# Every second context add moved from VectorE to GpSimd, and a window's input normalized in one pass, in a fused attention and feed-forward kernel

## The reference

```python
scores = jnp.einsum('nlcd,nled->nldce', q, k) / Kk ** 0.5
attn = jax.nn.softmax(scores, axis=-1)
ctx = jnp.einsum('nldcm,nlcd->nldm', attn, v)
ctx = ctx.transpose(0, 1, 3, 2)
out = jnp.einsum('nlck,ko->nlco', ctx, Wout) + bout
...
gated = jax.nn.silu(gate) * up
return jnp.einsum('bsh,dh->bsd', gated, w_down)
...
x = x + _layernorm(_L0_attn_ref(_layernorm(x, axis=-1), L0_attn_Wqkv, L0_attn_bqkv, L0_attn_Wout, L0_attn_bout), axis=-1)
x = x + _layernorm(_L0_ffn_ref(_layernorm(x, axis=-1), L0_ffn_w_gate, L0_ffn_w_up, L0_ffn_w_down), axis=-1)
```

## Time and profile before

| what | us |
|---|---|
| runs of the kernel before, median of 2 | 6556.85 (6422.88 and 6690.82) |
| profiled execution, its own time | 6414.95 |
| span of the profiled core (first to last instruction) | 6413.4 |
| spans of the 8 cores | 6396.5 to 6413.4 |
| VectorE busy | 3232.0 |
| TensorE busy | 3143.4 |
| ScalarE busy | 2046.3 |

### The profile page before, as it was taken

The page is one execution under the profiler, slowest core; times in us unless marked ns, Lnnn a source line. Parts: engine busy times, 40 slices in busy tenths (PEclk is TensorE's granted clock), DMA queues, the critical chain, the costliest instruction groups (busy, mean ns, idle before and its releaser), DMA issues.

```text
span 6413.4 us, 47482 instructions; the slowest of 8 cores (6396.5 to 6413.4 us)
## 1 busy us (share of the span) xinstructions
PE 3143.4 (49%) x15293; PEld 1477.7 (23%) x15544; DVE 3232.0 (50%) x3780; ACT 2046.3 (32%) x2977; POOL 16.4 (0%) x34
## 2 busy tenths in 40 slices
...
GB/s 111 110 109 108 110 102 0 7 5 2 17 20 138 73 141 79 129 79 32 75 137 69 132 95 102 67 48 95 103 100 97 125 79 66 53 145 137 154 138 82
DMA packets 177941, 556.83 MB, mean 87 GB/s; under 512 B 49568, under 2 KB 65952, under 8 KB 174496
## 3 DMA queue, kind: packets, MB, share of 16 engines
...
...
## 4 chain that ended last, share of the span: by engine, by line
PE 30%; DVE 27%; another core or an unknown queue 15%; issue 12%; ACT 10%; DMA 6%; DVEq 1%; SPq 0%; ACTq 0%
PE dps L415 10%; PE gps L353 9%; PE ups L363 7%; DVE es_sb L321 6%; DMA wd_sb<-wdc 4%; DVE zs_sb L762 4%; DVE es_sb L747 4%; DVE zs_sb L756 3%; DVE ctx_sb L330 3%; ACT kd_sb L262 2%; DMA x2s_sb<-x2h 2%; PE mps L189 1%; ACT v_sb L299 1%; ACT q_sb L299 1%
## 5 line engine op out<-in xcount | busy, mean ns | idle before, releaser
L353 PE MATMUL gps<-xn_sb,wg_sb 128*128 128x512 bf16 x4008 | 935.1, 384 | 104.5 <-DVE gated_sb L388 88.1
L415 PE MATMUL dps<-gated_sb,wd_sb 128*128 128x512 bf16 x4013 | 920.1, 384 | 93.5 <-DMA wd_sb<-wdc 54.3
L784 ACT ACTIVATE es_sb<-es_sb 128x4096 bf16<-128x4096 bf16 x256 | 922.1, 3602 | 8.8 <-DVE es_sb L747 8.8
L363 PE MATMUL ups<-xn_sb,wu_sb 128*128 128x512 bf16 x4016 | 920.3, 379 | 4.2
L249 PE MATMUL mps<-xn_sb,wqkv_sb 128*128 128x128 bf16 x512 | 72.3, 302 | 1437.6 <-DVE xn_sb L815 1386.4
L202 DVE TENSOR_SCALAR st_sb<-mps 1x128 f32<-1x128 f32 x48 | 13.3, 278 | 1429.5 <-PE mps L189 1429.5
L773 ACT ACTIVATE rz_sb<-zf_sb 128x128 bf16<-128x128 bf16 x256 | 79.0, 309 | 1855.0 <-DVE zf_sb L766 1854.8
L321 DVE TENSOR_TENSOR es_sb<-es_sb,u_sb 128x4096 bf16<-128x4096 bf16 x256 | 586.8, 2292 | 28.0 <-DVE u_sb L312 1.8
L747 DVE TENSOR_TENSOR es_sb<-q_sb,kd_sb 128x4096 bf16<-128x4096 bf16 x256 | 584.9, 2286 | 8.7 <-DVE ctx_sb L326 0.5
L330 DVE TENSOR_TENSOR ctx_sb<-ctx_sb,es_sb 128x4096 bf16<-128x4096 bf16 x240 | 550.1, 2292 | 24.9
L353 PEld LDWEIGHTS gps<-xn_sb,wg_sb 128*128 128x128 bf16 x4096 | 399.1, 99 | 611.4 <-issue 157.9
...
## 6 DMA issues: line engine op xcount, KB each, us to landing
wg_sb<-wgc SPq DMA_DIRECT2D x256, 512.0 KB, 3.7
wu_sb<-wuc SPq DMA_DIRECT2D x256, 512.0 KB, 3.7
wd_sb<-wdc SPq DMA_DIRECT2D x256, 512.0 KB, 3.4
...
```

The lines of the kernel that those rows point to most:

```text
L353: return tn.matmul(out=gps[pb].ap(), lhsT=wg_sb[pb].ap()[:, ft * 128:(ft + 1) * 128], rhs=xn2_sb.ap()[:, ft * W:(ft + 1) * W], start=(ft = ...
L363: return tn.matmul(out=ups[pb].ap(), lhsT=wu_sb[pb].ap()[:, ft * 128:(ft + 1) * 128], rhs=xn2_sb.ap()[:, ft * W:(ft + 1) * W], start=(ft = ...
L415: return tn.matmul(out=dps[pb].ap(), lhsT=wd_sb[wb].ap()[:, sh * 128:(sh + 1) * 128], rhs=gated_sb.ap()[:, ht * W:(ht + 1) * W], start=(ht ...
L784: ta = plan.op("A", lambda a, buf=buf: a.activation(out=buf.ap(), in_=buf.ap(), func=AF.Exp, scale=0.125), deps=[last[f"s_{c}_{j}"]], inc="A")
```

## The change

Three things are edited.

First, in `emit_uP` the add into `ctx_sb` of odd j is put into POOL's list; even j stay with VectorE. Each add still depends on the one before, and whatever reads the sum depends on it.

Second, the broadcast of the second normalization's rows is no longer made per chunk. VectorE copies the two rows of a chunk into `a2b2_w`, and the broadcast is made once for the whole window, two matmuls of 128x512 and two ScalarE evictions.

Third, `emit_xn2prep_early` and `emit_xn2prep_late` are replaced by one `emit_xn2prep`, called where the late part was. It loads all four quarters from `x2h` behind the spill of the window's last chunk and then runs 16 pairs of operations, each on 512 tokens.

```diff
@@ emit_uP
-        eng = "V"
+        eng = "V" if j % 2 == 0 else "G"
...
-    def emit_xn2prep_early(w):
+    def emit_xn2prep(w):
+        te = None
+        for half, dst in ((0, a2bc_sb), (1, b2bc_sb)):
+            b = next_mbank()
+            tk = plan.op("T", lambda tn, half=half, b=b: tn.matmul(
+                out=mps[b].ap()[:, 0:W], lhsT=ones_r.ap(),
+                rhs=a2b2_w.ap()[0:1, half * W:(half + 1) * W],
+                start=True, stop=True),
+                deps=dep(f"pm{b}") + [last[f"a2b2_{w}"]], inc="T")
+            te = plan.op("A", lambda a, b=b, dst=dst: a.activation(
+                out=dst.ap(), in_=mps[b].ap()[:, 0:W], func=AF.Copy),
+                deps=[tk] + dep("a2bcfree"), inc="A")
...
             def d_r(s, w=w, k=k):
                 src = x2h.rearrange("(fp p) tok -> p fp tok", p=128)[
-                    :, k:k + 1, w * W:w * W + 3 * T]
+                    :, k:k + 1, w * W:(w + 1) * W]
...
-            d = dep("xn2_free") + [last[f"spill_c{CPW * w + CPW - 2}"]]
+            d = dep("xn2_free") + [last[f"spill_w{w}"]]
             if k >= 4:
                 d.append(trs[k - 4])
             trs.append(plan.op("S", d_r, deps=d, inc=f"Dxr{k % 4}"))
...
-    def emit_xn2prep_late(w):
...
-            tk2 = plan.op("T", lambda tn, b=b: tn.matmul(
-                out=mps[b].ap()[:, 0:2 * T], lhsT=ones_r.ap(),
-                rhs=ab_row.ap(), start=True, stop=True),
-                deps=dep(f"pm{b}", "ones") + [t2], inc="T")
...
+            tcp = plan.op("V", lambda v, cl2=cl2: v.tensor_copy(
+                out=a2b2_w.ap()[0:1, cl2 * T:(cl2 + 1) * T],
+                in_=ab_row.ap()[0:1, 0:T]), deps=[t2] + dep("a2b2free"),
+                inc="V")
...
         if 0 <= c - 1 < NC and (c - 1) % CPW == CPW - 1:
-            emit_xn2prep_late((c - 1) // CPW)
+            emit_xn2prep((c - 1) // CPW)
...
-        if 0 <= c < NC and c % CPW == CPW - 1:
-            emit_xn2prep_early(c // CPW)
```

More of the change, by code:

```diff
@@ L539, in emit_fin @@
         last["outsfree"] = tw
-    def emit_xn2prep_early(w):
+    def emit_xn2prep(w):
[10 more added lines that the diff above has]
+                deps=[tk] + dep("a2bcfree"), inc="A")
+            last[f"pm{b}"] = te
+        ab2bc = te
+        last["a2b2free"] = te
         trs = []
@@ L554, in emit_xn2prep_early @@
         tv = None
-        abdep = [last[f"a2bc_{CPW * w + i}"] for i in range(CPW - 1)]
         for k in range(NFT):
-            xn2r = xn2_sb.ap()[:, k * W:k * W + 3 * T]
+            xn2r = xn2_sb.ap()[:, k * W:(k + 1) * W]
             tv = plan.op("V", lambda v, xn2r=xn2r: v.tensor_mul(
-                out=xn2r, in0=xn2r, in1=a2bc_sb.ap()[:, 0:3 * T]),
-                deps=[trs[k]] + abdep, inc="V")
+                out=xn2r, in0=xn2r, in1=a2bc_sb.ap()),
+                deps=[trs[k], ab2bc], inc="V")
             tv = plan.op("V", lambda v, xn2r=xn2r: v.tensor_sub(
-                out=xn2r, in0=xn2r, in1=b2bc_sb.ap()[:, 0:3 * T]),
-                deps=[tv], inc="V")
-        for i in range(CPW - 1):
-            last[f"a2bcfree{i}"] = tv
-    def emit_xn2prep_late(w):
-        cl = CPW - 1
-        xcv = x2c_sb.ap().rearrange("p (f t) -> p f t", f=NFT)
-        xnv = xn2_sb.ap().rearrange("p (f w) -> p f w", f=NFT)[
-            :, :, cl * T:(cl + 1) * T]
-        tcp = plan.op("V", lambda v, xnv=xnv, xcv=xcv: v.tensor_copy(
-            out=xnv, in_=xcv),
-            deps=dep("xn2_free") + [last[f"x2_{CPW * w + cl}"]], inc="V")
-        last["x2c_free2"] = tcp
-        tv = None
-        for k in range(NFT):
-            xn2r = xn2_sb.ap()[:, k * W + cl * T:k * W + (cl + 1) * T]
-            tv = plan.op("V", lambda v, xn2r=xn2r: v.tensor_mul(
-                out=xn2r, in0=xn2r,
-                in1=a2bc_sb.ap()[:, cl * T:(cl + 1) * T]),
-                deps=[tcp, last[f"a2bc_{CPW * w + cl}"]], inc="V")
-            tv = plan.op("V", lambda v, xn2r=xn2r: v.tensor_sub(
-                out=xn2r, in0=xn2r,
-                in1=b2bc_sb.ap()[:, cl * T:(cl + 1) * T]),
-                deps=[tv], inc="V")
-        last[f"a2bcfree{cl}"] = tv
+                out=xn2r, in0=xn2r, in1=b2bc_sb.ap()), deps=[tv], inc="V")
+        last["a2bcfree"] = tv
         last[f"xn2_{w}"] = tv
@@ L675, in build_program @@
                 out=x23, in0=xb3, in1=sq3, op=ALU.add),
-                deps=[tv] + dep("x2c_free", "x2c_free2")
-                + [last[f"xb{cp}"]], inc="V")
+                deps=[tv] + dep("x2c_free") + [last[f"xb{cp}"]], inc="V")
             last["ao_free"] = tv
```

21 lines of the change are left out of this document (7 added, 14 removed).

## The result

The changed kernel took 6917.56 us (median of 11 runs, 6831.57 to 7003.31) against 6416.87 us (10 runs) before. The ratio is 1.0683, 95% interval 1.064 to 1.0725, 6.8% slower; it leaves out the executions in which some cores showed a lower TensorE clock and took a few per cent longer, as the two medians don't.

A forecast was written before the change was run, and what follows sets the result against it. The prediction took VectorE's in-order stream as the chain in nearly all of slots 0 to 15. Its terms summed to +494 us on the profiled execution's 6415 us, giving 6909 us, 7.7% slower, with an 8-in-10 range of 6550 to 7250 us.

The forecast's parts named there:

- The hold: Odd attention steps: next score product waits 9.2 us for POOL's add; +188 attention alone, +117 gate/up, +70 last odd steps.
- Rival B: POOL's add takes 5.5 us, the unpacked rate, so gate/up steps hide it; +145 us, 6560 us; chance 15%.
- C: Not slower: POOL adds at VectorE's rate, 2.3 us; 6371 us together; chance 5%.
- The two engines together: VectorE operations on two SBUF tiles beside POOL's add: cost taken midway between undisturbed and one behind the other; +45 and +35 us.
- slot ends: Step 15's POOL add beside xn1's two operations at 15 ends: between -2.3 and +6.9 us each, middle +2.3, +35 us.
- output steps: Twelve steps with fin operations beside POOL's add: between +1 or less and +6.9 us each, 3.7 taken, +45 us.
- rival A: VectorE work on two SBUF tiles and a POOL add exclude each other; +6.9 us per place, 7016 us; chance 28%.
- Steps with down atoms: Eighteen feed-forward down-projection steps beside attention: slack nearly hides POOL's add, 1.0 us charged each, +18 us.
- Broadcast: No broadcast per chunk: ScalarE is free sooner, 12 slot ends that aren't a window's come 1.9 us earlier, -23 us.
- One-pass preparation: xn2 prepared in one piece behind the window's last chunk: +4.5 us at each of 4 windows, +14 us together.
- TensorE's clock: 39 odd gate/up steps: longer idling drops the clock to 1.2 GHz in one of three, 13 x 1.8, +23 us.
- Rival D: TensorE stays at 1.2 GHz for every whole odd gate/up step, 28.0 us each; 7268 us; chance 7%.

The follow-up runs named there:

- run 3: The changed kernel with only the add of each slot's last step, step 15, back on VectorE; ratio to the kernel before 1.0538.
- run 7: The kernel before with only the chunk's broadcast emitted behind the next chunk's sums, at the 12 slot ends closing no window; ratio to before 0.9967.

## Why the prediction came out right, step by step

The direction and the size were right: +494 us predicted, +424 measured, 6909 us against 6838.6 for the profiled execution, with the mechanism named as the largest term in its place. But two of its sizes were off in opposite directions, and what I gave 28% as a rival is what happens.

- **The hold.** Right in mechanism, mis-sized in its price. I took POOL's add as 8.93 us, from an f32 operation of VectorE on 128 elements; it takes 7.93 us, and with the hand-over 8.2. That a row of VectorE on 128 elements came within 13% of it was luck, since no row tied the two engines. With this number the prediction's own subtractions give 5.7, 2.0 and 4.8 us (8.2 less 2.5, 6.2 and an average of 3.4 between P and the next score product); measured are 5.65, 1.98 and 4.92. One wrong microsecond, 79 times, is 79 of the 375 us of these three terms. Rival B, 5.5 us, falls with this number, and so does C.
- **The two engines together.** This was the open place, and I took the middle between undisturbed and shut out, at the slot ends and at the output steps. The middle was wrong: it is the full exclusion, rival A. Slot ends cost 5.2 us each in place of 2.3, 42 us more, and run 3 shows it by taking away the neighbour. The output steps cost 5.0 and not 3.7. With the add at 7.93, A's own 6.9 us become 5.9 (8.2 less 2.3). The slot ends stay 0.7 under that since L792 and the hand-over to POOL overlap: the add that stood for L792 is only 0.8 us longer (the 8757 ns above) than one that stood for nothing. The rule stood in the prediction, with rival A: the Trainium skill, page "SBUF — State Buffer", section "Who interferes with whom", says that a VectorE instruction with two SBUF inputs and a GpSimd instruction that reads SBUF shut each other out for the whole instruction. By that rule the trace agrees, with 8.74 us for L796, and with L383, which reads one operand from PSUM, at most 0.69. The middle between the ends left 56 us out.
- **Steps with down atoms.** I had +18, measured are -14. The even steps gave back 64 us and the odd ones took 50: TensorE runs through such steps at its own pace, and the late VectorE catches up in the next. That the slack of two steps is one account is what I wrote; I then charged 1.0 us a step all the same.
- **Broadcast.** -23 predicted, -22 in the changed kernel and -24.6 in run 7. That the sums wait for ScalarE's square, and this for the two evictions, held.
- **One-pass preparation.** +4.5 us a window predicted, +7.9 measured. The step that failed: I let the last load set the end, with two operations behind it. VectorE at the end of window 0:

```profile
2086.70 0.42 DVE L571 TENSOR_TENSOR xn_sb<-xn_sb,a2bc_sb 128x512 bf16<-128x512 bf16 x1 [3.41 <-DMA xn_sb<-x2h]
2087.23 0.42 DVE L574 TENSOR_TENSOR xn_sb<-xn_sb,b2bc_sb 128x512 bf16<-128x512 bf16 x1
...
2100.34 0.42 DVE L574 TENSOR_TENSOR xn_sb<-xn_sb,b2bc_sb 128x512 bf16<-128x512 bf16 x1
2100.68 0.27 DVE L202 TENSOR_SCALAR st_sb<-mps 1x128 f32<-1x128 f32 x1
```

and SyncE's queue there:

```profile
2076.21 0.36 SPq L689 DMA_DIRECT2D x2h<-x2c_sb  x1
2081.98 12.24 SPq L561 DMA_DIRECT2D xn_sb<-x2h  x16
```

  VectorE waits once, for the first load, and then needs 14.0 us for its own 32 operations (2086.70 to 2100.68), more than the 12.2 in which the loads are issued. It is 24.5 us from the spill to L202, where I had 20.3 (1903.67 to 1924), worked out from the queue of the earlier trace rows. What I had forecast as waits of about 10 us at L571 is one of 3.4. (By its own rows the prediction's weight loads would be issued from 1920.4 on and not from 1920.8; nothing hangs on it.)
- **TensorE's clock.** +23 predicted, about nothing measured. The drops came, more often than I said: in the steps of slots 4 to 15 TensorE idled 25 times for 3.0 to 5.5 us ahead of gate/up or down matmuls, and 24 times the granted clock fell to 0.50 for a short while, late in the stretch or within 1.3 us behind it. One of them in the timeline, and the window of 4 us around it (PEclk is the third number from the end):

```profile
2165.82 4.96 PE L353 MATMUL gps<-xn_sb,wg_sb 128*128 128x512 bf16 x16 [5.03 <-DVE gated_sb L388]
```

```profile
2164.00:2168.00 4.00, 2.17 (x6) 0.81 (x7) 2.77 (x5) 2.35 (x4) 0.00 (x0) 0.65 0.00 0
```

  Sixteen matmuls took 4.96 us in place of 3.62, which is 1.3 us lost and not the 3 that I took, and VectorE is the pace there anyway. The 27 odd gate/up steps with a low clock somewhere in them take 17.2 us at the median, as do the 12 without; of the even ones the 29 with and the 13 without take 15.2. The step that failed is the last subtraction, 3 us lost of which only 1.2 fit into slack: less was lost, and all of it fitted. Rival D falls too: odd gate/up steps stayed at 17.2, not 28.0.

So the closeness of the sum is partly luck: the hold was too dear by 79 us, clock and down steps by 55, and the exclusion and the windows were too cheap by some 66.

What stays open: whether the exclusion needs both operands of VectorE in SBUF, or goes with something else that L796, L524 and L737 have in common and L383 and L388 haven't. They also differ in pace, 0.6 to 0.8 ns an element (1.22 us for 2048, 0.42 for 512) against 1.3 (0.69 for 512). L383 and L388 have one operand in SBUF and one in PSUM; no run put a copy or another operation with its only input in SBUF beside POOL's add.
